# Two-layer attention and feed-forward kernel: the stores of the quantized weights go from SyncE's queue to GpSimd's, and the loads that refill their buffers wait for other things

## What is computed

```python
x = L0_attn_x                                  # [8, 2048, 1024] f32
xn = layernorm(x)
x = x + L0_attn(xn, ...) + L0_ffn(xn, ...)     # layer 0: decayed linear attention + int4-quantized dense + rank 16 part
xn = layernorm(x)
x = x + L1_attn(xn, ...) + L1_ffn(xn, W1, b1, W2, b2)
# L1_ffn: both weights are made ternary first
gamma = mean(abs(W));  Wq = clip(round(W / (gamma + EPS)), -1, 1)     # W1: [4096, 1024], W2: [1024, 4096]
h = relu(x @ Wq1.T + b1);  out = h @ Wq2.T + b2
```

## Time and profile before

| what | us |
|---|---|
| median of two timed runs (1603.13 and 1803.88) | 1703.51 |
| the profiled execution, its own time | 1598.82 |
| its span on the slowest core (8 cores: 1571.6 to 1597.3) | 1597.3 |
| TensorE busy | 1234.9 |
| ScalarE busy | 474.9 |
| VectorE busy | 419.7 |
| GpSimd busy | 66.6 |

### The profile page before, as it was taken

One profiled execution on the slowest core, in us unless ns is written; L12 is line 12 of the kernel. 1 busy time (PEld: TensorE's weight loads), 2 busy tenths in 40 slices (PEclk: granted clock), 3 DMA queues, 4 the chain that ended last, 5 costly groups with the idle time before them and its releaser, 6 DMA issues. The chain is left out here.

```text
span 1597.3 us, 15226 instructions; the slowest of 8 cores (1571.6 to 1597.3 us)
## 1 busy us (share of the span) xinstructions
PE 1234.9 (77%) x5332; PEld 534.6 (33%) x5440; DVE 419.7 (26%) x704; ACT 474.9 (30%) x550; POOL 66.6 (4%) x97
## 2 busy tenths in 40 slices
PE   0275289996597587765469499979997999889997
PEld 0121034442233232222124144434443444334443
DVE  1497435003223324333265200021002200031000
ACT  1564033334324526636023142013202140031400
POOL 3331100000000000000100000000000000000000
PEclk9988589998798887887779799989998999989999
DMA  8795952003335647758660644234433053231522
GB/s 194 115 170 87 134 79 52 1 0 106 97 88 191 177 121 234 192 189 224 125 100 1 158 132 158 106 132 112 152 119 144 31 153 133 95 116 48 189 107 105
DMA packets 135963, 194.43 MB, mean 122 GB/s; under 512 B 74032, under 2 KB 82256, under 8 KB 131536
## 3 DMA queue, kind: packets, MB, share of 16 engines
q1 hardware_dynamic: 108224, 138.43, 28.3%
q0 software_dynamic: 27664, 55.00, 17.7%
HBM read 195.57 MB, written 33.56 MB: 143 GB/s over the span
## 5 line engine op out<-in xcount | busy, mean ns | idle before, releaser
L1200 PE MATMUL pb<-bigA,wqA 128*128 128x512 bf16 x1002 | 224.8, 379 | 1.2
L1160 PE MATMUL pb<-xn,xbf 128*128 128x512 bf16 x1004 | 221.5, 380 | 1.1
L1143 PE MATMUL pb<-stm,bigB 128*128 128x512 bf16 x627 | 145.3, 391 | 43.3 <-DVE xa_bf L1016 35.8
L1101 ACT ACTIVATE bigA<-pb,biasL,sc 128x512 bf16<-128x512 f32 x128 | 99.5, 777 | 219.2 <-PE pb L1160 219.2
L1182 PE MATMUL pb<-rt,projW 128*128 128x512 bf16 x501 | 125.4, 391 | 40.8 <-DVE rt L1021 35.8
L1051 DVE SCALAR_TENSOR_TENSOR xf<-pb,biasL,xf 128x512 f32<-128x512 f32 x32 | 24.0, 751 | 479.5 <-PE pb L1200 479.5
L1160 PEld LDWEIGHTS pb<-xn,xbf 128*128 128x128 bf16 x1024 | 100.2, 98 | 121.7
L1200 PEld LDWEIGHTS pb<-bigA,wqA 128*128 128x128 bf16 x1024 | 100.2, 98 | 120.8
L1130 PE MATMUL pb<-xn 128*128 128x512 bf16 x313 | 78.8, 415 | 49.1 <-PEq L933 28.1
L681 PE MATMUL pb<-projW,xn 128*128 128x512 bf16 x503 | 112.1, 382 | 0.5
L1143 PEld LDWEIGHTS pb<-stm,bigB 128*128 128x128 bf16 x640 | 63.4, 100 | 125.2 <-issue 55.9
(11 more groups left out here) (131 smaller groups left out, 978.6 us busy)
## 6 DMA issues: line engine op xcount, KB each, us to landing
xbf<-W1qS SPq DMA_DIRECT2D x128, 256.0 KB, 2.7
wqA<-W2qS SPq DMA_DIRECT2D x32, 1024.0 KB, 4.8
xbf<-W2T SPq DMA_DIRECT2D x26, 512.0 KB, 4.4
bigA<-W2T POOLq DMA_DIRECT2D x32, 256.0 KB, 9.3
bigA<-W1T POOLq DMA_DIRECT2D x16, 512.0 KB, 9.6
xf<-xT SPq DMA_DIRECT2D x4, 2048.0 KB, 8.5
x1S<-xf POOLq DMA_DIRECT2D x4, 2048.0 KB, 8.2
stm<-W1T SPq DMA_DIRECT2D x16, 512.0 KB, 5.6
```

The source lines that it names most:

```text
L1101: got = si(s.activation(bigA[:, fc * 512:(fc + 1) * 512], pb[fc % 2][:, :], AF.Relu, bias=biasL[:, 48 + fc:49 + fc], scale=sc[:, C_Q4:C_Q4 ...
L1143: got = ti(t.matmul(bank[:, :], bigB[:, i * 1024 + ec * 128: i * 1024 + (ec + 1) * 128], stm[:, i * 512:(i + 1) * 512], start=(n == 0), st ...
L1160: got = ti(t.matmul(bank[:, :], xbf[:, (fc % 4) * 1024 + dc * 128: (fc % 4) * 1024 + (dc + 1) * 128], xn[:, p0:p0 + TS], start=(dc == 0), ...
L1200: got = ti(t.matmul(bank[:, :], wqA[:, (dc % 2) * 4096 + fc * 128: (dc % 2) * 4096 + (fc + 1) * 128], bigA[:, fc * 512:(fc + 1) * 512], st ...
```

## The change

Three things change in the blocks of layer 0, and the names of semaphores elsewhere follow.

- The 64 stores of quantized pieces are issued by GpSimd, in a loop ahead of its x1S store. For each piece it waits for the combine; from the fifth piece of a block on it first waits for the store four pieces earlier to have landed. The loads stay on SyncE.
- SyncE no longer waits for combines. It issues the refill of a slot as soon as the store out of that slot has landed, whatever the next piece's combine does.
- The stores use the semaphores sDi, sDj, sDk, sDl in place of sDc, sDd, sDg, sDh, and the later waits for them name these.

```diff
@@ attn_tile
-                return [(qcD, sDc), (qdD, sDd), (qgD2, sDg), (qhD2, sDh)][h % 4]
+                return [(qiD, sDi), (qjD, sDj), (qkD, sDk), (qlD, sDl)][h % 4]
+
+            qst_keys = ["di", "dj", "dk", "dl"]
+            exp_qst = [Q[qst_keys[h % 4]] + 16 * (h // 4 + 1) for h in range(NH)]
@@ attn_tile, SyncE
                     for h in range(min(NSL, NH)):
                         q_qld[h] = qld_q(h)[0](s, qldF(h), q_src(h))
-                    for h in range(NH):
-                        s.wait_ge(sV, cmb_tok[h])
-                        q_qst[h] = qst_q(h)[0](s, q_dst(h), qout(h))
-                        hl = h - 1 + NSL
-                        if h >= 1 and hl < NH:
-                            s.wait_ge(qst_q(h - 1)[1], q_qst[h - 1])
-                            q_qld[hl] = qld_q(hl)[0](s, qldF(hl), q_src(hl))
+                    for h in range(NSL, NH):
+                        s.wait_ge(qst_q(h - NSL)[1], exp_qst[h - NSL])
+                        q_qld[h] = qld_q(h)[0](s, qldF(h), q_src(h))
@@ attn_tile, GpSimd
             def _(g):
+                if layer == 0:
+                    for h in range(NH):
+                        if h >= 4:
+                            g.wait_ge(qst_q(h - 4)[1], q_qst[h - 4])
+                        g.wait_ge(sV, cmb_tok[h])
+                        q_qst[h] = qst_q(h)[0](g, q_dst(h), qout(h))
                 g.wait_ge(sV, v_res[7])
                 dst = x1S if layer == 0 else outT
                 qgD(g, tile_dst(dst, j), xf[:, :])
```

More of the change, by code:

```diff
@@ L576, in _ @@
                     g.wait_ge(sQg, qg_snap)
[L577 to L580, removed]
+                    g.wait_ge(sDi, Q["di"])
+                    g.wait_ge(sDj, Q["dj"])
+                    g.wait_ge(sDk, Q["dk"])
+                    g.wait_ge(sDl, Q["dl"])
                 qfn0 = [qiD, qjD]
@@ L950, in _ @@
                         q_qld[h] = qld_q(h)[0](s, qldF(h), q_src(h))
-                    for h in range(NH):
-                        s.wait_ge(sV, cmb_tok[h])
-                        q_qst[h] = qst_q(h)[0](s, q_dst(h), qout(h))
-                        hl = h - 1 + NSL
-                        if h >= 1 and hl < NH:
-                            s.wait_ge(qst_q(h - 1)[1], q_qst[h - 1])
-                            q_qld[hl] = qld_q(hl)[0](s, qldF(hl), q_src(hl))
+                    for h in range(NSL, NH):
+                        s.wait_ge(qst_q(h - NSL)[1], exp_qst[h - NSL])
+                        q_qld[h] = qld_q(h)[0](s, qldF(h), q_src(h))
                     fin = {}
                     for h in range(NH):
-                        fin[qst_q(h)[1].name] = (qst_q(h)[1], q_qst[h])
+                        fin[qst_q(h)[1].name] = (qst_q(h)[1], exp_qst[h])
                     QCARRY["fin"] = list(fin.values())
@@ L963, in _ @@
                     if j == 0:
[L964 to L967, removed]
+                        s.wait_ge(sDi, Q["di"])
+                        s.wait_ge(sDj, Q["dj"])
+                        s.wait_ge(sDk, Q["dk"])
+                        s.wait_ge(sDl, Q["dl"])
                     for fc in range(NFC):
@@ L1209, in _ @@
             def _(g):
+                if layer == 0:
[4 more added lines that the diff above has]
+                        q_qst[h] = qst_q(h)[0](g, q_dst(h), qout(h))
+                        assert q_qst[h] == exp_qst[h], (h, q_qst[h], exp_qst[h])
                 g.wait_ge(sV, v_res[7])
```

## The result

The changed kernel takes 0.9936 of the time before [0.9918, 0.9955], some 10 us less (medians 1594.65 of 12 runs and 1732.93 of 11; part of the executions of both kernels, up to 1811 us, ran on disturbed cores, and the ratio leaves them out). Measured again on two other chips it was 0.996 [0.9946, 0.9973] and 0.996 [0.9944, 0.9976], 6.4 us less. These ratios are of 1593.1, 1592.8 and 1592.9 us for the changed kernel and 1603.3, 1598.8 and 1600.3 for the kernel before. What makes the first gain the larger one is thus the kernel before, and why it took longer there is open. The forecast was 3.8 us less. The time predicted, 1595.0, stands beside 1590.54 for the profiled execution. The sign was right and the gain is larger.

What follows compares the result with a forecast made beforehand. Bound taken: TensorE waiting for the quantizer, which is short of loaded pieces, 71.6 of 1598.8 us. Tile terms -4.6 - 1.5 - 2.0 + 1.3 + 3.0 = -3.8 us give 1595.0; range 1580 to 1626.

Steps and rivals of the forecast that it cites:

- turns: Time from a piece's combine to its slot's refill issue; forecast 3.9 us for W2qS stores, 4.7 for W1qS; ten counted.
- rival B: Loads also get quicker, no longer close behind a store in their queue; 1.0 from ten loads gives 1585; chance 0.15.
- The landing: GpSimd's stores of quantized pieces land in 3.3 us to W2qS and 4.1 to W1qS.
- Tile 0: Two slots: piece 4's second turn falls from 8.46 to 3.9 us, -4.6; the stall at the first res, -1.5.
- Tile 1: Three slots, four turns to piece 12: the long one, 6.8 us, loses 2.9; -2.0 taken for the tile.
- Tile 2: Four slots, two turns to piece 11: the second goes from 3.6 to 4.7 us; +1.3 for the tile.
- Tile 3: Four slots, two turns to piece 8: from 2.9 and 3.5 us, both to 4.7; together +3.0.
- Each microsecond on the turn is 10 us: Ten turns lie on the paths of the four tiles, so each microsecond per turn is about 10 us of time.
- Rival A: GpSimd's stores land late, 1.8 to 2.2 us more per turn, costing 18 to 22: 1615; chance 0.25.
- Rival C: ScalarE and VectorE work in order, so early loads only wait for their place: +4, 1603; chance 0.1.
- The stretched issues: GpSimd's DMA issues lengthened beside VectorE, 0.9 at most each; +9 us if at ten turns, counted as none.
- What costs nothing: SyncE's 64 lost issues, GpSimd's 64 added ones and the barrier behind the x1S store: no effect on time.

Runs made afterwards that it cites:

- r1: Changed kernel, but each refill also waits for the next piece's combine, as before the change; 1.001 of the time of the kernel before.
- r7: Changed kernel without the 64 stores, a refill waiting only for its slot's combine; one execution 1572.96 us, beside 1599.61 for the kernel before.
- r6: Changed kernel with four memsets and drains on GpSimd ahead of each store; 1.0282 of the time of the kernel before.
- r2: Changed kernel with stores back on SyncE, which waits for each landing and refills at once; 1.0172 of the time of the kernel before.
- r8: Tile 0 with SyncE storing, waiting for the landing and refilling at once, tiles 1 to 3 as before the change; 0.9928 of the kernel before.
- r5: Tile 0 with SyncE storing and refilling right behind the landing, tile 1 as changed, tiles 2 and 3 as before; 0.9924 of the kernel before.
- r9: Against the kernel before, roles swapped: SyncE issues stores behind combines, GpSimd waits for landings and issues refills; 0.9985 of its time.

## Why the prediction was right and wrong

The prediction sums turns. The last combine that TensorE waits for (piece 4 in tile 0, ahead of xa; pieces 12, 11 and 8 in tiles 1 to 3, ahead of the last R) stands at the end of one slot's rounds: first load, sign passes and combine, turn, load, and so on. Here is that chain, mean over the cores of the profiles of the table, before and changed, in us:

| tile | turns | forecast for the turns | loads behind the turns | first load | all the rest | last combine, from the block's start |
|---|---|---|---|---|---|---|
| 0 | 12.7, 7.6 (-5.1) | -4.6 | 9.3, 8.0 (-1.3) | 9.8, 9.8 | +0.1 | 46.4, 40.1 (-6.3) |
| 1 | 17.9, 17.7 (-0.2) | -2.0 | 18.5, 16.9 (-1.7) | 9.1, 8.9 | +0.4 | 65.6, 64.0 (-1.6) |
| 2 | 8.7, 11.5 (+2.8) | +1.3 | 10.8, 10.0 (-0.8) | 11.7, 11.1 | +0.6 | 49.9, 51.8 (+1.9) |
| 3 | 6.8, 9.3 (+2.5) | +3.0 | 11.0, 9.8 (-1.2) | 9.3, 8.9 | +0.3 | 38.0, 39.1 (+1.2) |
| sum | 0.0 | -2.3 | -5.0 | -1.2 | +1.4 | -4.8 |

With the 1.6 us that tile 0 gains at its first res this makes -6.4 of the -6.6 us. The turns cancel: tile 0 gains what tiles 2 and 3 lose. What is left as the gain are the loads. **The step that failed is the one that left the load at its 4.4 us**: rival B's mechanism, given a chance of 0.15 and nothing in the sum. It came at half its price, 0.5 us for each of ten loads, 5.0 in sum. I had written that the turn is the only part of the loop that the change touches. The second term off are the turns of tiles 1 and 2, in sum 3.3 us longer than worked out. Without the decoupling there is no gain (r1), since nothing then pays for the longer turns. The 10 us of the first measurement are some 3.5 more than the blocks give, and no term of the prediction or of this table accounts for that.

- **What bounds the kernel: right.** With the turn gone (r7) the three blocks are 29 us shorter. The first two groups of waits had said where TensorE stood, and the third why.
- **GpSimd's start and issue: right**, 0.54 and 0.89 us. **The landing: right in tile 0 alone**, where it took 3.2 to 3.3 and the turn 3.8 (worked out: 3.9). It doesn't go with the tensor, as I had it (3.3 to W2qS, 4.1 to W1qS), but with the piece loads in flight when the store is issued: 3.2 us with none, 3.8 with one, 4.8 with two or more (medians of all stores). Tiles 1 to 3 have more slots and so more loads in flight, and a turn on the path took up to 5.5 in tile 1 and 6.1 in tile 2.
- **Tile 0, -6.1 against -8.1 measured.** The stall at the first res went as forecast (-1.6 against -1.5), and the stall for xa fell to 9.6 where I had said about 11.5. Of the term of 4.6 us the turn of piece 2 gave 4.9 (8.7 to 3.8), the turn of piece 0 another 0.2, and the load of piece 4 another 1.3 (it landed in 5.1 us before and in 3.8 now). I had taken that load as unchanged. Before, it was issued 0.45 us behind a store on the same queue. But so were its neighbours, pieces 3, 5 and 6, which landed in 4.2 to 4.5 us. Without any store (r7) it took 3.8, as in the change. So the store ahead explains 0.4 to 0.7 us, and why piece 4's load took 0.6 to 0.9 more than its neighbours' is open.
- **Tile 1: the number right by luck** (-2.0 against -1.8). The long turn lost 0.5 us and not 2.9, since the store now lands in 4.8 us there; the four turns in sum hardly moved, and the loads gave the gain (-1.7).
- **Tile 2: +1.3 against +2.1.** The sign and place were right (the stall at the first res, 10.1 to 12.4). Two turns of 5.5 and 6.1 us, where 4.7 was worked out, cost 2.8, and the loads gave back 0.8.
- **Tile 3: +3.0 against +1.2.** The turns grew by 2.5 us in the mean, near the forecast (on the slowest core by 0.9 and 2.9). The loads gave back 1.2 and the first load 0.4. Loaded pieces did not wait for their place in ScalarE's list: it began pieces 4 and 8 within 0.25 us of their landing in both kernels.
- **Each microsecond on the turn is 10 us: near, and a little high.** Down to no turn it was 0.8 for each microsecond (r7: 29.3 for 36.8), upwards 0.7 in tile 0 (r6: 2.6 for 3.6).
- **Rival A, late landings: in part.** Landings of 4.2 to 5.9 us (pieces 3 and 7 in tile 2, piece 4 in tile 3) reach its upper value of 5.1, and make these tiles lose. In tile 0 the landing was the one worked out.
- **Rival B, quicker loads: at half its price, and it decided the size of the gain.** The medians show little of it (W2T 4.4 to 4.1, W1T from 5.5 to 5.2 into xbf and 5.6 into stm as before), the loads on the paths more. r1 has it too (-5.0 us), so it came with the stores' leaving SyncE's queue; but r2 and r8 have it in tile 0 with the stores on SyncE and 2.7 us ahead of the load (3.8 and 3.7 us for piece 4). Whether queue or spacing makes it in tiles 1 to 3 is not shown.
- **Rival C, that early loads are of no use: refuted** by tile 0, and by r1, which takes the early issue away and loses the gain.
- **The stretched issues, counted at none: right.** All 64 took 0.88 to 0.91 us on every core. The Trainium skill (SBUF — State Buffer, "SBUF: two separate sides") has GpSimd stall in building descriptors beside certain modes of VectorE. No issue in these blocks shows it, with the combines and the products with the masks running on VectorE throughout.
- **What costs nothing: right.** The wait at the barrier was 29.0 us after 29.8.

## What to carry to other kernels

When a queue both issues a store and waits for landings, price two things: the turn of a buffer, and the pace at which the queue can serve pieces when it sits out each wait in order. Here, with two buffers the turn decides, and one queue that waits and refills at once was best; with four the pace decides, and then the queue that refills one piece late, as before, was best, and two issuers came next. So the best order can differ between stages of one kernel: r5 gives each block its own and takes 0.9924 of the time, against 0.9936 to 0.996 for the change made everywhere (measured on other chips, each against the kernel before). Most of that is tile 0: r8, which changes no other, has 0.9928.

And where a sum of turns comes out near nothing, price the transfers between them too. Half a microsecond on each load, ten times on the path, was most of what this change gained in the end.

## What the runs showed of the hardware

- The same store makes far fewer packets from GpSimd. Against the page before (108224 packets on the hardware queue, 27664 on the software queue) the 64 stores took 66560 off the one and put 5120 on the other, 1040 and 80 for each. The engines' time fell as well, from 28.3 + 17.7 = 46.0% to 45.1%. The Trainium skill (DMA: Bandwidth & Descriptors, "SWDGE vs HWDGE vs iDMA") has a GpSimd packet hold up to 64 descriptors and preferably 4096 B at most; 256 KB in 4 KB packets are 64, so the 80 agree but for 16. The store still landed 0.6 us later by the medians (W2qS, 3.4 against 2.8), about what its longer issue takes (0.89 against 0.36).
- The landing of a 256 KB store goes with the 512 KB loads in flight when it is issued. Over all cores of the three profiles of the changed kernel the medians are 3.2 us with none, 3.8 with one and 4.8 with two or more; with none they are 3.2 for every kind of store, to either tensor and from xbf or stm. SyncE's stores in the two profiles of before took 2.8, 3.4 and 4.4. This is a count over the traces, not an experiment of its own.
- A drain on GpSimd behind a DMA issue held the engine for 2.1 us (r6), where one behind a memset alone held it for 0.2.
- In tile 0 of the kernel before, the loads of pieces 2 to 11, each issued 0.45 us behind a store of its own queue, landed in 4.2 to 4.8 us (means over the cores), and that of piece 4 in 5.1. Where no store stood less than 2.6 us ahead of it (the change, r2, r8), piece 4's took 3.7 to 3.9, and 3.8 without any store (r7).
- The load of x took 12.2 us beside piece loads from the other queue against 8.3 ahead of them in its own (r9), and the first piece load of tile 0 then landed in 7.6 us in place of 9.8. The Trainium skill (DMA: Bandwidth & Descriptors, "SWDGE vs HWDGE vs iDMA") says that DMAs issued by GpSimd and those of SyncE feed different queues inside each DMA engine, which serves them in turn. The two loads of r9 agree, and order in one queue was worth 4 us to that of x.
